# A decoder kernel with hand-laid tables: a new order of steps on five engines and of its PSUM pairs

## The chip, the cores and the metric

The kernel runs on one core of a Trainium2 chip. The core has a tensor engine (TensorE, PE in the profile; its weight loads are PEld), a vector engine (VectorE, DVE), a scalar engine (ScalarE, ACT), GpSimd (POOL), and a sync engine (SyncE, SP) that here only issues DMA transfers. Each runs its own instruction stream in order; they meet at semaphores. The metric is the device time of one execution, in microseconds (us). Lower is better.

## The reference, cut to what matters

Four decoder layers of three sublayers each are applied to `x` (64 sequences, 128 tokens, 128 channels). Each sublayer is followed by a residual and a layer norm:

```
x = _layernorm(x + _L0_attn_ref(x, ...))      # linear recurrence with a delta rule
x = _layernorm(x + _L0_xattn_ref(ctx_1024, x, ctx_1024, ...))   # 16 heads of 8 channels, 77 context rows
x = _layernorm(x + _L0_ffn_ref(x, gate_w, w1, w2))              # 8 experts, top 32 tokens each
x = _layernorm(x + _L1_attn_ref(...))         # 8 heads of 128, latent keys and values, causal
x = _layernorm(x + _L1_xattn_ref(...))        # cross attention with a mask
x = _layernorm(x + _L1_ffn_ref(...))          # fp4 quantized gate, up and down
...                                           # L2: attention, cross attention, mixture with low-rank tokens
...                                           # L3: rotary attention, relu cross attention,
                                              #     conv + attention + 8 gated experts of width 512
```

Nothing of this computation is changed. The same instructions run before and after.

## The kernel before

A first phase, the opening (about 375 us), solves the recurrence's triangular systems for all sequences and prepares weights. It isn't touched. Then comes the decoder phase. It takes the 64 sequences as 16 batches of 4. Three groups of buffers (`g0`, `g1`, `g2`, class `Group`) are in use at once: group n works through batches n, n+3, n+6, ..., one after another, and each visit is a *turn*. Group 0 has six turns, the other two have five.

Each engine's work on a batch is a Python generator that yields after each *step*: a few instructions that end with an increment of the group's semaphore for that engine. `whole_tensor`, `whole_scalar`, `whole_vector`, `whole_gpsimd` and `whole_sync` string the batches of a group together. The order in which an engine takes the three groups' steps is not found by a planner at build time. It stands in a table, `ORDER`: a digit per step says whose step comes next, and `in_order` obeys:

```
def in_order(programs, order):
    for who in order:
        next(programs[who], None)
```

So within one group the steps never change places. Only how the three groups are interleaved on an engine is free. SP has five programs: the three groups' loads and stores (digits 0, 1, 2) and two streams of expert weights, `a` for layer 0 and `b` for layer 3 (`stream_sync`, line 3044), 256 KB a piece into four places each. A piece waits until the matmuls that read the place's last content are done. Since SP runs in order, whatever stands behind a waiting step waits too.

At the end of a turn the group's SP program does these steps in this order: the store of the output (`store_sync`, L3024, after the last layer norm, "end normal"), then the next batch's loads (`loads_sync`): key mask (L2995), the dots (L2998), the context (L3002), the transposed input xT (L3006, into `qa`), the recurrence's result z in four DMAs (L3011) and the input x (L3015, into `o`).

On TensorE the new turn starts with *rec v* (L1764), which waits for xT, then *rec q* (L1767), *rec weights* (L1772, also waits for z and for ScalarE), and *rec y* (L1778). GpSimd adds a bias to x (*rec base*, L1843), VectorE adds rec y to it (*rec sum*, L1377), and the layer norm follows.

The attention sublayers use the same steps for each of 4 sequences: scores (L1599), two row maxima on VectorE (L1703), tops turned (L1611), scores shifted by the maximum (L1626), two exponentials on ScalarE (L1679), weighted values (L1649), by tokens (L1660). Lines 1599 and 1626 use 32 rows of the array per matmul and L1649 32 columns; the others use all of it, in the profile `128*128`. L2759 to L2806 are the gated experts of the last layer, L1986 and L1996 the experts of the first.

The second table, `GIVEN`, is a list of pairs of digits. It hands four pairs of PSUM banks in turn to the stages of the three groups (`give_banks`); a stage's first matmul waits until the pair's last reader is done (`take_banks`).

Of the kernel before, what the change touches and what calls it, by code (L numbers as in the profile page):

```python
# [224 lines left out]
def memory_layouts(w):  # L225
# [39 lines left out]
        "00101010202010210120020000201000010200020010110010112121211121221211121212201012012002100022000200010010"  # L265
        "00102021010000101101121121010100100101121101011001100100012020201001101101012002010121010211012212121111"
        "21120112021012201001021220220002102220210002010012102212211212111121222121112122211021002002020002222101"
        "12212110110122202020212012122020202220200202220202001202110100001001001010011010010100110101000110110110"
        "00110120012010220221221012001011010010111010201010110102111211000001011102120021010010101000101210100010"
        "20002020001211010110220212112221211212221211122012010011101221012101012020020202000220202000222020110120"  # L270
        "12202101220210102110010102021010001001100100200100201002000101000100200100100102001000002010010000010000"
        "10010010000212122121121210021021011011011010111021102011101100101110110002101110100011011002010101111102"
        "01101211010110010021001020021100120020020200000201102111102200002002220020020002010210020100120112020201"
        "01020120021021001011010010111010001011101001010211000122222101020210020020202211222211201122112102022112"
        "10100210201110101101200201211022000102202100012022002022021020201220120202220220020222020002202220200022"
        "02200101022022122011002101121021120110120120120210112011010102112212212212010000101121222111101001011101"
        "00221012100022020220002022001210120112011012100200222021222212010220021011021201010100101101000101110100"
        "01011102120121011021202212212222022122012102210022022022011002100200100110100100010010121002001020210020"
        "02120010010020010020022002212211021221201202012020212012212102102121002100200200200122112111222212121222"
        "12121212001011100101001110100112012212212022012010110001012020002101002112201201012121211212212111212221"  # L280
        "21112121220102102212020100002000201200120012021100100121021211210121110210012112012111211212021002001202"
        "01212112101011201220120020102102120120102002112110212010210001011011012012110121102102211011002020200002"
        "00002202001210122211212112221211202002120020012010122112110212101021121202110201201120202022020020222020"
        "00202220200012012010202011211011011011211210111012022101210201202212122102221020220220221022122000121202"
        "20212101202022022212112212211011002102120120110120210201102101010101122122122212012221001101022012211101"
        "01011101010101220200022020220002002012101012101210121202020220102212102202010212101202201010100101101000"
        "10111010001011102021020101221112022022202210122010220120120210200200202002200020010012010001001010102120"
        "01201110210021021012100100200212011021221202200102212210201201221221220122102102000200200200121212111222"
        "21212122212121212001010110101001110100112012210021221202211011000120020121001201210202010012121211212212"
        "11121222121112122210101210122002200000020202001021002021002101022120100102101112212110110211021012212112"  # L290
        "01121020121121121010110110210122010201012012020020121121201200121201200101100110111011201021202002021101"
        "10002022020002022101210222012112121221212122012002010012000122121112102111101021120122002012120202022020"
        "02022202000202220200022101201020011211111101121102101112021111211021102120220022021222102200202202220120"
        "00120212010122020220222122011001202102101102210110110220210210210210112221212211201202210221212021001121"
        "22210111101011101010101220202002020220002022100101021011201211202222000201212221020220201011021201010100"
# [149 lines left out]
    "13001223231122100203202011110223122302112002230020030221202001122112130302231102110002101200110321000013"  # L445
    "03222111122310022311212110102312030122102203101312212103200300212300011022232311021020021001012302100112"
    "12001103001321222111120012032301231020231210222011130220020121011312012022022000010022010000011301012300"
    "2300220223230300")

# [3053 lines left out]
```

## Time and profile before

| | |
|---|---|
| median of 3 runs | 5209.06 us (5198.81 to 5213.58) |
| the profiled execution | 5213.06 us |
| its span, first to last instruction | 5211.0 us |
| PE, DVE, ACT, POOL busy | 88%, 63%, 48%, 15% |
| PE busy from 420 us on | 4332.10 of 4791.00 us |

Busy shares count instructions in execution. In the decoder phase TensorE is nearly always busy, and the others wait for it and it for them in turn. The granted clock of TensorE is given as a share of full speed.

### The profile page before, as it was taken

What the parts mean: (1) busy time and instruction counts of PE and PEld (TensorE: products, weight loads), DVE (VectorE), ACT (ScalarE), POOL (GpSimd) and SP (SyncE); (2) the same over time, 40 slices, a digit from 0 to 9 for tenths busy, and PEclk for the clock granted to TensorE, in tenths of its full rate; (3) what the DMA queues carried; (4) which work ended last, traced back from release to release, by engine and by line L of the source; (5) the groups of instructions that cost most, each with busy time, mean ns of one, the idle gap of its engine ahead of it and who ended that gap; (6) DMA issues with size and microseconds to landing.
All of it is one profiled execution on the core that took longest, in us unless ns stands there. A gap on an engine that the chain in (4) does not pass through costs nothing.

```text
span 5211.0 us, 128498 instructions
## 1 busy us (share of the span) xinstructions
PE 4591.7 (88%) x54601; PEld 3382.8 (65%) x54601; DVE 3270.9 (63%) x8433; ACT 2486.6 (48%) x5062; POOL 786.2 (15%) x841
## 2 busy tenths in 40 slices
PE   5668988999898989899898989999998989898877
PEld 4336756677676767676676767676676767676554
DVE  6654587655657575756757575756657575757552
ACT  3324655535545455544545454544545454554431
POOL 5551210111011110101011111101011111101000
PEclk7668999999999999999999999999999999999987
DMA  2131100012010101111010101011000101010000
GB/s 65 29 89 51 61 2 2 4 55 59 28 34 19 56 21 48 29 40 37 22 42 15 56 21 50 25 44 35 26 30 21 56 23 50 23 40 24 14 23 29
DMA packets 154184, 181.62 MB, mean 35 GB/s; under 512 B 62890, under 2 KB 82450, under 8 KB 152850
## 3 DMA queue, kind: packets, MB, share of 16 engines
q1 hardware_dynamic: 153618, 173.41, 11.2%
q8 instruction: 437, 7.16, 0.6%
q14 instruction: 129, 1.06, 0.1%
HBM read 162.50 MB, written 10.55 MB: 33 GB/s over the span
## 4 chain that ended last, share of the span: by engine, by line
PE 66%; DVE 14%; ACT 6%; issue 3%; DMA 1%; POOL 1%; SPq 1%; POOLq 0%; DVEq 0%; ACTq 0%
PE g_pair L2774 9%; PE g_pair L2759 9%; PE g_pair L1599 6%; PE g_pair L1649 5%; DVE g_tops L1703 5%; PE g_pair L1626 5%; ACT g_keys_exps L1679 3%; PE g_pair L1996 2%; PE g_pair L1986 2%; PE g_pair L1433 2%; PE g_pair L1611 1%; PE g_pair L1660 1%; PE g_pair L2360 1%; PE g_pair L2060 1%; PE g_pair L1569 1%
## 5 line engine op out<-in xcount | busy, mean ns | idle before, releaser
L1679 ACT ACTIVATE g_keys_exps<-g_pair 128x1024 f32<-128x1024 f32 (+1 forms) x768 | 746.4, 1018 | 570.6 <-PE g_pair L1626 569.1
L1703 DVE TENSOR_REDUCE g_tops<-g_pair 128x8 f32<-128x1024 f32 (+1 forms) x768 | 749.9, 1006 | 335.1 <-PE g_pair L1599 332.8
L1412 POOL TENSOR_TENSOR g_rstd<-g_rstd,minus_half 128x4 f32<-128x4 f32 x224 | 234.8, 1049 | 3325.2 <-DVE g_rstd L1394 3319.0
L2774 PEld LDWEIGHTS g_pair<-region,g_keys_exps 128*128 128x128 f32 x4096 | 510.5, 192 | 120.1 <-issue 109.7
L2759 PE MATMUL g_pair<-g_xT,region 128*128 128x512 f32 x1024 | 545.1, 614 | 8.5 <-ACT g_keys_exps L2787 4.5
L2774 PE MATMUL g_pair<-region,g_keys_exps 128*128 128x128 f32 x4096 | 547.5, 278 | 2.9 <-DVE g_base L2806 2.9
L1649 PE MATMUL g_pair<-g_keys_exps,g_v 77*32 77x128 f32 (+1 forms) x12288 | 438.2, 286 | 70.6 <-DVE g_tops L1703 62.6
L1626 PE MATMUL g_pair<-g_qa,g_keys_exps 32*77 32x128 f32 (+1 forms) x12288 | 449.6, 284 | 46.0 <-DVE g_o L1724 28.7
L1599 PE MATMUL g_pair<-g_keys_exps,g_qa 32*128 32x256 f32 (+1 forms) x6144 | 394.1, 371 | 96.9 <-ACT g_keys_exps L1679 80.2
L1626 PEld LDWEIGHTS g_pair<-g_qa,g_keys_exps 32*77 32x77 f32 (+1 forms) x12288 | 386.1, 171 | 142.9 <-DVE g_o L1724 58.9
L1649 PEld LDWEIGHTS g_pair<-g_keys_exps,g_v 77*32 77x32 f32 (+1 forms) x12288 | 328.3, 114 | 178.9 <-DVE g_tops L1703 118.4
L1599 PEld LDWEIGHTS g_pair<-g_keys_exps,g_qa 32*128 32x128 f32 x6144 | 262.3, 192 | 206.5 <-ACT g_keys_exps L1679 130.9
L2787 ACT ACTIVATE g_keys_exps<-g_pair,region 128x512 f32<-128x512 f32 x256 | 176.0, 688 | 445.5 <-PE g_pair L2759 445.0
L2799 DVE TENSOR_SCALAR g_keys_exps<-g_pair,region 128x512 f32<-128x512 f32 x256 | 191.1, 747 | 308.5 <-PE g_pair L2759 308.0
L1673 ACT ACTIVATE g_oT_sc<-g_pair 128x256 f32<-128x256 f32 x384 | 147.1, 383 | 322.3 <-PE g_pair L1649 321.6
L1706 DVE TENSOR_TENSOR g_qa<-g_qa,g_pair 128x256 f32<-128x256 f32 x384 | 160.7, 419 | 201.9 <-PE g_pair L1611 199.4
L1421 ACT ACTIVATE g_x<-g_x,g_shift,g_rstd 128x128 f32<-128x128 f32 x384 | 173.0, 489 | 173.3 <-DVE g_shift L1398 173.0
L2155 POOL TENSOR_TENSOR g_keys_exps<-g_keys_exps,g_small 128x512 f32<-128x512 f32 x128 | 133.6, 1064 | 549.9 <-DVE g_small L2180 549.8
L2139 ACT ACTIVATE g_keys_exps<-g_pair,g_small 128x128 f32<-128x128 f32 x512 | 180.4, 379 | 52.3 <-DVE g_small L2169 51.7
L1611 PE MATMUL g_pair<-consts_sb,g_tops 128*128 128x128 f32 x768 | 159.5, 290 | 50.8 <-DVE g_tops L1703 47.9
L2759 PEld LDWEIGHTS g_pair<-g_xT,region 128*128 128x128 f32 x1024 | 157.8, 192 | 49.3 <-issue 41.2
L1660 PE MATMUL g_pair<-consts_sb,g_oT_sc 128*128 128x128 f32 x768 | 163.5, 299 | 21.8 <-ACT g_keys_exps L1679 11.2
(379 smaller groups left out, 8554.2 us busy)
## 6 DMA issues: line engine op xcount, KB each, us to landing
region<-L_w_in SPq DMA_DIRECT2D x512, 256.0 KB, 3.0
region<-xT_in SPq DMA_DIRECT2D x16, 256.0 KB, 2.7
z_scratch<-m_z SPq DMA_DIRECT2D x4, 1024.0 KB, 5.9
g_qa<-xT_in SPq DMA_DIRECT2D x16, 256.0 KB, 3.9
g_oT_sc<-z_scratch SPq DMA_DIRECT2D x64, 64.0 KB, 3.2
g_o<-x_in SPq DMA_DIRECT2D x16, 256.0 KB, 3.8
out<-g_x SPq DMA_DIRECT2D x16, 256.0 KB, 2.3
setup_weights<-prepared_in SPq DMA_DIRECT2D x1, 2589.5 KB, 10.6
```

Source lines behind the costliest of these rows:

```text
L1412: e.tensor_tensor(g.rstd[:, :], g.rstd[:, :], g.s["minus_half"], ALU.pow).then_inc(*b.gpsimd(st + " rstd"))
L1599: ins = e.matmul(bank[r][:, 2 * nk * t:2 * nk * (t + 1)].rearrange("p (i k) -> p i k", i=2), g.qa[rows, t, n, :], g.km[rows, n, t, :, 0:nk ...
L1611: ins = e.transpose(bank[2][:, t * T:(t + 1) * T], top_rows(g, t), g.k["ident"])
L1626: ins = e.matmul(bank[r][0:nk, u * T:(u + 1) * T], g.km[rows, n, t, i, 0:nk], g.qa[rows, t, n, :], start=not masked, stop=not masked or u ...
L1649: ins = e.matmul(b.bank[st][0][32 * u:32 * u + 32, k * T:(k + 1) * T], g.v[0:nk, n, 8 * i + 4 * k + u, :], g.p[0:nk, 2 * i + k, u, :], sta ...
L1660: ins = e.transpose(b.bank[st][1][:, k * P:(k + 1) * P], outputs_of(g, n)[:, k, :], g.k["ident"])
L1679: e.activation(g.p[0:nk, 2 * k:2 * k + 2, :, :].rearrange("p g u q -> p (g u q)"), b.pair[st][k][0:nk, :, :].rearrange("p r c -> p (r c)") ...
L1703: e.tensor_reduce(top_columns(g, k), src, AX, ALU.max).then_inc(*b.vector(f"{st} top {n} {k}"))
L2139: ins = e.activation(g.lat_e[n % 2][:, j, :], bank[2 + kv][:, h * T:(h + 1) * T], ACT.Exp, bias=g.small[:, 40 + j:41 + j], accum_out=g.lat ...
L2759: e.matmul(bank[0][:, :], weights.part(f"w1 {x}", c), g.xT, start=True, stop=True).then_inc(*b.tensor(f"f3 hidden {k}"))
L2774: ins = e.matmul(bank[1][:, n * D:(n + 1) * D], g.gated_hid[:, x % 2, c, n * T:(n + 1) * T], weights.part(f"w2 {x}", c), start=c == n == 0 ...
L2799: e.tensor_scalar(g.gated_hid[:, x % 2, k % HC, :], b.bank["ex"][0][:, :], g.w["f3_b1"][:, k:k + 1], 0.0, ALU.add, ALU.max).then_inc(*b.ve ...
```

## The change

All entries of `ORDER` and `GIVEN` are laid anew; no function is touched. The tables keep their length and the count of each digit: 5040 steps on TensorE, of which 1353 places hold another digit, 971 of 3472 on ScalarE, 2456 of 7728 on VectorE, 134 of 528 on GpSimd, 173 of 624 on SP. A step stands on average half a place (TensorE) to two places (SP's loads) from where it stood. One line of SP's table stands for all:

```diff
     "sync": (
-        "00002212aa12abb01112ba0b21aaaaaaaaaaaaaaaaaaaaaaaaaaaaaaaaaaaaaaaaaaaaaaaabbbbbbbbbbbbb000bb0000bbbbbbbb"
+        "00000111120b22a21ba2a1a2aaaaaaaaaaaaaaaaaaaaaaaaaaabaaabaaaaaaaaaaaaaaaaaabbbbbbbbbbbbb000000bb0bbbbbbbb"
...
 GIVEN = (
-    "02201102112003221303110211030213200323111011002203012220101201031220010013122301221001110201231120231110"
+    "00201102032011132203111120020313020311102311002222002313120101001201231013012011020223120320022112131102"
```

**SP at the decoder's start.** `g0`, `g1`, `g2` are the groups; `region` is the place of weight pieces. Before, from the eleventh issue on:

```order
L3006 DMA g2_qa<-xT_in 128x512
L3054 DMA region<-L0_w1_in 128x512
L3054 DMA region<-L3_w1_in 128x512 x2
L3011 DMA g0_oT_sc<-z_scratch 128x4x32 x4
L3002 DMA g1_ctxT<-ctxT_in 128x308
L3006 DMA g1_qa<-xT_in 128x512
L3011 DMA g1_oT_sc<-z_scratch 128x4x32 x4
L3011 DMA g2_oT_sc<-z_scratch 128x4x32 x4
L3054 DMA region<-L3_w2_in 128x512
L3054 DMA region<-L0_w1_in 128x512
L3015 DMA g0_o<-x_in 128x4x128
```

This piece is preceded by ten more issues (g0's mask, dots, context and xT, small loads of g1 and g2, two weight pieces). After, from the very first issue to the same load of g0's x:

```order
L2995 DMA g0_mask_int<-key_mask_in 1x308
L2998 DMA g0_kq_dot<-s_scratch 128x4
L3002 DMA g0_ctxT<-ctxT_in 128x308
L3006 DMA g0_qa<-xT_in 128x512
L3011 DMA g0_oT_sc<-z_scratch 128x4x32 x4
L2995 DMA g1_mask_int<-key_mask_in 1x308
L2998 DMA g1_kq_dot<-s_scratch 128x4
L3002 DMA g1_ctxT<-ctxT_in 128x308
L3006 DMA g1_qa<-xT_in 128x512
L2995 DMA g2_mask_int<-key_mask_in 1x308
L3015 DMA g0_o<-x_in 128x4x128
```

Group 0's z and x have moved ahead of the loads of group 2 and of all weight pieces: x is the eleventh row instead of the twenty-first.

**TensorE at the decoder's start.** Before, from its first matmul (`g_pair` are PSUM pairs):

```order
L1764 MATMUL g_pair2<-rec_vo,g0_qa 128x128 x4
L1767 MATMUL g_pair2<-g0_qa,region 128x512
L1764 MATMUL g_pair1<-rec_vo,g1_qa 128x128 x4
L1772 MATMUL g_pair2<-g0_qa,g0_oT_sc 128x128 x4
L1767 MATMUL g_pair1<-g1_qa,region 128x512
L1778 MATMUL g_pair2<-g0_keys_exps 128x128 x4
L1772 MATMUL g_pair1<-g1_qa,g1_oT_sc 128x128 x4
L1474 MATMUL g_pair2<-g0_ctxT,region 128x308
```

After:

```order
L1764 MATMUL g_pair0<-rec_vo,g0_qa 128x128 x4
L1767 MATMUL g_pair0<-g0_qa,region 128x512
L1772 MATMUL g_pair0<-g0_qa,g0_oT_sc 128x128 x4
L1764 MATMUL g_pair1<-rec_vo,g1_qa 128x128 x4
L1778 MATMUL g_pair0<-g0_keys_exps 128x128 x4
L1474 MATMUL g_pair2<-g0_ctxT,region 128x308
```

Group 0's rec weights (L1772) stands ahead of group 1's rec v (L1764), and its rec y (L1778) ahead of group 1's rec q (L1767). Group 0 has changed its pair from 2 to 0.

**SP at the end of a turn**, here group 1's first. Before; the store is the third row:

```order
L3054 DMA region<-L3_w1_in 128x512
L3054 DMA region<-L0_w2_in 128x512 x7
L3024 DMA out<-g1_x 128x4x128
L3054 DMA region<-L3_w1_in 128x512
L3054 DMA region<-L3_w2_in 128x512
L2995 DMA g1_mask_int<-key_mask_in 1x308
L2998 DMA g1_kq_dot<-s_scratch 128x4
L3054 DMA region<-L0_w1_in 128x512 x2
L3002 DMA g1_ctxT<-ctxT_in 128x308
L3006 DMA g1_qa<-xT_in 128x512
L3054 DMA region<-L0_w1_in 128x512
```

After:

```order
L3054 DMA region<-L3_w2_in 128x512
L3054 DMA region<-L0_w1_in 128x512
L3024 DMA out<-g1_x 128x4x128
L3054 DMA region<-L0_w1_in 128x512 x2
L2995 DMA g1_mask_int<-key_mask_in 1x308
L2998 DMA g1_kq_dot<-s_scratch 128x4
L3002 DMA g1_ctxT<-ctxT_in 128x308
L3006 DMA g1_qa<-xT_in 128x512
L3011 DMA g1_oT_sc<-z_scratch 128x4x32 x4
```

Between the store (L3024) and the load of xT (L3006) stood four weight pieces (L3054), now two. Over the 13 ends of a turn that are followed by another turn, 23 pieces stood there before and 5 now. The result's load z (L3011) follows xT at once, and the weight pieces come after it.

## Rows read from the trace of the kernel before

**Rows 1.** Busy time by stretch: start:end, length, busy per engine, clock, DMA share, GB/s
```profile
410.00:700.00 290.00, 256.20 (x3010) 198.20 (x3009) 172.54 (x457) 161.14 (x404) 43.83 (x40) 0.89 0.15 45
...
1600.00:2200.00 600.00, 549.38 (x6565) 410.86 (x6564) 394.53 (x1040) 309.72 (x593) 74.86 (x70) 0.99 0.11 34
```

**Rows 2.** Who waited for whom: total us, times, longest us
```profile
PE g_pair L1599 <- ACT g_keys_exps L1679: 80.2, 99, 3.4
...
PE g_pair L1649 <- DVE g_tops L1703: 62.6, 125, 1.8
...
PE g_pair L1611 <- DVE g_tops L1703: 47.9, 50, 2.5
```

**Rows 3.** The same for 420 to 5211 us, TensorE and the first-input load
```profile
PE g_pair L1764 <- DMA g_qa<-xT_in: 31.6, 13, 5.0
```

**Rows 4.** Timeline of SP, group 1's first turn: start, us, line, tiles
```profile
1265.62 0.39 SPq L3024 DMA_DIRECT2D out<-g_x  x1
1266.06 0.99 SPq L3054 DMA_DIRECT2D region<-L_w_in  x2
...
1269.23 0.43 SPq L3006 DMA_DIRECT2D g_qa<-xT_in  x1
...
1271.01 2.62 SPq L3011 DMA_DIRECT2D g_oT_sc<-z_scratch  x4
```

**Rows 5.** Timeline of TensorE there; in brackets the idle time before
```profile
1274.76 2.08 PE L1764 MATMUL g_pair<-rec_vo,g_qa 128*128 128x128 f32 x8 [5.00 <-DMA g_qa<-xT_in]
```

**Rows 6.** Timeline of SP, group 0's last turn: no weights in between
```profile
4502.78 0.40 SPq L3024 DMA_DIRECT2D out<-g_x  x1
...
4504.49 0.43 SPq L3006 DMA_DIRECT2D g_qa<-xT_in  x1
```

**Rows 7.** Timeline of TensorE there
```profile
4507.41 1.16 PE L1764 MATMUL g_pair<-rec_vo,g_qa 128*128 128x128 f32 x8 [1.17 <-DMA g_qa<-xT_in]
```

**Rows 8.** Chain that ended last: start, us, what
```profile
1269.23 5.48 DMA g_qa<-xT_in
...
2454.99 6.28 DMA g_qa<-xT_in
```

**Rows 9.** By stretch: 4 us after the load landed, four turns of the thirteen
```profile
1130.20:1134.20 4.00, 3.91 (x16) 2.76 (x17) 0.00 (x0) 0.69 (x1) 1.40 (x2) 0.62 0.55 155
1274.70:1278.70 4.00, 3.94 (x44) 3.45 (x44) 1.83 (x4) 0.00 (x0) 0.00 (x0) 0.60 0.65 157
...
2165.00:2169.00 4.00, 3.93 (x25) 2.91 (x26) 0.71 (x2) 0.00 (x0) 1.67 (x3) 0.57 0.40 92
...
3927.80:3931.80 4.00, 3.95 (x14) 2.45 (x18) 1.02 (x3) 0.13 (x1) 0.30 (x1) 0.50 0.72 203
```

**Rows 10.** Chain at the decoder's start: start, us, what
```profile
391.56 4.02 DMA g_o<-x_in
...
395.65 1.10 POOL g_base L1843
...
396.85 0.70 DVE g_x L1377
```

**Rows 11.** Timeline of TensorE at the start
```profile
377.88 2.04 PE L1764 MATMUL g_pair<-rec_vo,g_qa 128*128 128x128 f32 x8 [7.39 <-DMA g_qa<-xT_in]
...
387.95 2.04 PE L1764 MATMUL g_pair<-rec_vo,g_qa 128*128 128x128 f32 x8 [6.32 <-DMA g_qa<-xT_in]
389.79 1.92 PE L1772 MATMUL g_pair<-g_qa,g_oT_sc 128*128 128x128 f32 x8
...
393.20 1.38 PE L1778 MATMUL g_pair<-g_keys_exps 128*128 128x128 f32 x8
```

**Rows 12.** Timeline of TensorE in a full stretch
```profile
2022.87 1.06 PE L2774 MATMUL g_pair<-region,g_keys_exps 128*128 128x128 f32 x8
...
2025.58 1.11 PE L1626 MATMUL g_pair<-g_qa,g_keys_exps 32*77 32x128 f32 x32
2026.62 1.16 PE L2774 MATMUL g_pair<-region,g_keys_exps 128*128 128x128 f32 x8
```

More of the change, by code:

```diff
@@ new lines @@
+        "12210112021012210100201220200022012220120002010012122012211212111121222121112122121021002002002020220121"
+        "12212110110122221020022012122020202220200202220200021202110100001001001010011010010100110101000110110110"
+        "00110102012010220221221012001011010010111021001010110102112111000001011102120021010010120100010110100010"
+        "20020020001211010110220212112221211212221212112010100111201221012101012020020202000220202000222020101121"
+        "02021201222010120110010102021010001001100102001002000102000100100102001000001010020001002000100100010010"
@@ L313 @@
+        "22220000002220220022020002202000202202000000002022020000000000000000000000000000000000000000000000000000"
         "000000000000000000000000000000000000000000000000"),
     "scalar": (
[L315 to L317 removed]
@@ new lines @@
+        "01100120120120222100011111111100022222120020102100012221222222210110102000112010211120020000000202211111"
+        "02112201022220111011111110002222201200102200011221222222221011002001011021021211002000000002221211111021"
+        "22012202010111111111000022221220201210000221221222222101100002011012102111202000000000222121101112201212"
+        "22010011111111100020222212200012100021221222222121110002000112010211210002000000202211202220220200000002"
+        "02000000"),
+    "sync": (
+        "00000111120b22a21ba2a1a2aaaaaaaaaaaaaaaaaaaaaaaaaaabaaabaaaaaaaaaaaaaaaaaabbbbbbbbbbbbb000000bb0bbbbbbbb"
+        "bbbbbaabaaaaaaaaaaabba1aa11111b1aaaaaaaaaaaabbbabababbbbbbabbbbb2222222aaaaaaaaaaaabbbbbabbabbbbab00000b"
+        "00abbbaaaaaaaaaaaabababbbbabbbbbb11a1111bb1bbaaaaaaaaaaaaababbbbbbaabbbbb222222bb2bbaaaaaaaabaaaaaabbbba"
+        "abbbbbbbbbb0000000baaaaaaaaaaaabbbaababbbbabbbbb11111b1bb1aaaaaaaaaaaababbaabbbbbbbbbb222222b2bbaaaaaaaa"
+        "aaaaababbbabbbbbaabbb000000bbb0baaaaaaaaaaaabaabbbbbaabbbbbb1b11b11bb11aaaaaaaaaaababaaabbabbbbbbbbbb222"
+        "222b2baaaaaaaaaaaabaabababbbbbbbbb0000000bbaabaaaaaaaaaabbbbbbbbbbbbbbbbb1bbbbbbbbbbbbbbbb2bbbbbbbbbbbb0"),
@@ L452 @@
+    "21130012012110211310230223211012011010220301221123122320012301000123001022001112000123232201001212230110"
+    "11120022032100130003221211231112002311221223102101201301201302112220232002021103230221002100000101002322"
+    "2301010200000300")
 BATCH = {
```

327 lines of the change are left out of this document (154 added, 173 removed).

## The prediction

> **What bounds the kernel now.** I first read the busy shares by stretch. From 420 us on TensorE is busy 4332 of 4791 us, in a typical stretch 549 of 600 us at a granted clock of 0.99 [rows 1]. So TensorE bounds the kernel. The matmuls themselves can't go; what a new order can take away is TensorE's 459 us of idle time after 420 us (4791.00 - 4332.10, the table of the section on time), the idle time of the start, and time in which TensorE runs at less than its full clock.
>
> Next I read who waits for whom. The idle time is spread thin. The largest entries are the scores waiting for ScalarE's exponentials, 80.2 us in 99 waits, and weighted values and tops waiting for VectorE's maxima, 62.6 and 47.9 us in 125 and 50 waits [rows 2]. These are hand-overs inside an attention, half a microsecond to a microsecond each. One entry is of another kind: rec v, the first matmul of a new turn, waits for the load of xT in all 13 later turns, 31.6 us together, up to 5.0 us at once [rows 3].
>
> Then I read SP's timeline at such a place. The store of group 1's output is issued at 1265.62, two weight pieces stand behind it (0.99 us for the two), two more further on, and xT is issued only at 1269.23, 3.6 us after the store [rows 4]. TensorE idles 5.00 us for it [rows 5]. In the turn in which nothing stands between, the way from store to xT is 4504.49 - 4502.78 = 1.7 us, the matmul starts 2.9 us after the issue, and TensorE idles 1.17 us [rows 6, 7]. Between weight pieces the load itself is slower too: 5.48 and 6.28 us from issue to landing in the chain [rows 8].
>
> The wait has a second price. rec v after the wait of 5.00 us takes 2.08 us for its eight matmuls, after the wait of 1.17 us it takes 1.16 [rows 5, 7]. The stretches of 4 us behind the landing show the granted clock: 0.62, 0.60, 0.57 and 0.50, the lower of TensorE's two levels (1.2 GHz) for part or all of the time [rows 9]. Seven of the 13 turns show this, four of them with 0.50; the other six stay at 1.00.
>
> **The change part by part.** No instruction is added or removed, and the steps of one group keep their order, so every term is about time between steps.
>
> *Loads at the end of a turn.* Of 23 weight pieces that stood between store and xT over the 13 turns, 5 are left. Each took about 0.47 us of SP (0.99 for two plus the gap [rows 4]), so xT is issued 18 x 0.47 = 8.5 us earlier in sum, and without their traffic it should land in 2.9 us rather than 5.5 to 6.3 [rows 7, 8]. rec v also moved on TensorE. I counted in both orders, with the trace's duration of each step, the matmuls between the last step on which the store depends and rec v: 5.5 us on average before (3.7 to 6.6), 7.2 after (6.6 to 8.2). The way that this has to cover is 1.7 + 2.9 = 4.6 us in the undisturbed case [rows 6, 7], plus up to 1 us for the last normalization steps. 6.6 us cover it in every turn. So the idle 31.6 us can go whole, and with it the low clock: over 4 us each, 4 x (0.38 + 0.40 + 0.43 + 4 x 0.50) = 12.8 us [rows 9]. Together 44 us at most. I don't take it whole. While TensorE stood, VectorE and ScalarE caught up with their queues, and some of the hand-overs behind rec v will now be late in its place: the bounds are 0 and 44, and since the attention hand-overs in flight there are of 0.5 to 1 us (80.2/99, 62.6/125 [rows 2]), about one per turn, I give back 13 x 1.0 = 13 us and take -31 us.
>
> The Trainium skill weighs against part of this. Its page "DMA: Bandwidth & Descriptors", section "Anatomy of one DMA", puts a DMA's time at a fixed 2.0 us, mostly its completion, and bytes over 436 GB/s, measured for DMAs issued by GpSimd; for 256 KB that makes an estimate of 2.6 us whatever stands around it. The undisturbed landing agrees, those of 5.48 and 6.28 us don't [rows 7, 8], and the measurement decides. By the rule only the issue and the cover would count, and the turn at 2451, whose cover stays at 6.6, would keep some 2 us of its wait; the sum would be about 3 us smaller.
>
> *The start.* Group 0's x was issued at 391.56, landed 4.02 us later, and the chain of waits runs through it: bias on GpSimd 1.10 us, rec sum at 396.85 [rows 10]. It is now the eleventh SP step. From its present start the first four issues end at about 375.3; z's four take 2.6 (as in [rows 4]), five small ones about 0.4 each. That gives an issue near 379.8, landing near 383.8, bias done by 385. On TensorE rec v and rec q end at 381.6; then rec weights 1.92, rec v of group 1 about 2.0 and rec y 1.38 us follow [rows 11], the end is near 387.3. rec sum would start at 387.4 rather than 396.85: 9.5 us earlier. Up to 700 us TensorE is busy 256.20 of 290.00 us [rows 1], so what follows is partly bound by TensorE and not by this chain. I take -7 of bounds 0 and -10. The first two uses of pair 0 (group 0, then group 2) now follow each other, so group 2's rec v waits for rec sum; before it ran after 398, so this is covered.
>
> *Changes of array shape.* The order has 1897 neighbours of unlike shape (whole array, 32 rows, 32 columns) where it had 1921. A group of eight matmuls behind a 32-row group takes 1.16 us, behind others 1.06 [rows 12]. 24 x 0.10 = -2 us. With a row going into the 32-row shape costing as much again it is -5; zero is the other bound.
>
> *Everything else.* 1353 of TensorE's places changed, nearly all by a swap with a neighbour. I compared the cover (matmul time between a step and the step that waits for its result) by kind: scores behind the exponentials 1.93 us before and 1.96 now in the own attentions, tops turned 2.58 and 2.61, x0 to x2's weighted values 1.68 and 1.52. Waits for a hand-over with under 1 us of cover are 788 where they were 750. That is a wash: 0, with bounds from -20 to +20 (38 more by 0.5 us each, rounded [rows 2]). The weight pieces that now come after z have at least 7.4 us of matmuls before their use in layer 3, and landed in about 3: nothing.
>
> Sum: -31 - 7 - 2 = -40 us. The profiled execution took 5213.06 us, its span 5211.0; minus 40 is 5173. That execution lies 4.0 us above the median of the runs, 5209.06, so the median becomes **5169 us**. This measurement can't tell less than about 0.3% (16 us) from no change.
>
> **The rivals.**
> *The waits only move.* TensorE reaches the next hand-over earlier and waits there. For it: ScalarE and VectorE work through the same queues, and some waits of [rows 2] are bound by their chains. Against it: they are less loaded than TensorE, and the clock comes back in any case. If three quarters of the 31.6 us are given back and half of the clock's 12.8 remains, the gain is 8 + 6, with 2 for the start: -16, 5193 us, with a range to 5209.
> *Slower: thin covers break.* The place is scores against VectorE's maxima in the attentions. 38 more hand-overs have under 1 us of cover. If each exposes its longest of 1.8 us [rows 2] instead of 0.5, that is +68 against -40: 5237 us. It decides from 40/38 = 1.05 us each. Against it is that the mean of 125 such waits is 0.5.
> *More than that.* The small hand-overs improve as well, because the order was laid around real durations: 10% off 459 us of idle time, -46, with the -40: 5123 us. Against it: the covers are alike.
> *The tables don't do what they say,* no effect of waits and loads: 5209. The order speaks against it, since SP's loads have moved; I count it with the first rival.
>
> **How the numbers follow.** The forecast case (5150 to 5190) gets 0.58, the larger gain 0.12, the moved waits 0.20, the slower case 0.10. The best sum by the bounds is -44 - 10 - 5 - 20 = -79, 5130; the range takes most of that and the first rival: 5138 to 5206. Faster by over 0.3% (under 5193.4) has the forecast, the larger gain and a fifth of the moved waits: 0.74. Within 0.3%: 0.16. Slower: 0.10.
>
> **What would show it.** In the profile after, the waits of L1764 for xT fall from 31.6 us to under 8 from 420 us on, and the stretches behind them show a clock of 1.00. At each end of a turn SP issues xT 1.7 us after the store, where no weights stand between. At the start rec sum begins near 387, and TensorE's busy share up to 700 us rises. The waits of L1599, L1649 and L1611 stay within a tenth of 80, 63 and 48 us. If the xT waits are gone and those have grown by 25 us or more, the first rival is right; if they have grown by over 40, the slower one. If xT still lands late, my landing time of 2.9 us is wrong.

## The result, and the profile after

| | before | after |
|---|---|---|
| median | 5205.02 us (4 runs, 5198.81 to 5213.58) | 5134.37 us (4 runs, 5133.33 to 5134.58) |
| ratio, with its 95% interval | | 0.9863 [0.9846, 0.9880] |
| the profiled execution | 5213.06 us, span 5211.0 | 5134.53 us, span 5132.4 |
| PE busy from 420 us to the end | 4332.10 of 4791.00 us | 4293.94 of 4712.40 us |

The change takes off 71 us. The forecast was 40, and 5134.4 lies just under the range of 5138 to 5206. The profiled execution of before was 8 us slower than its median, so the two traces differ by 79 us. From 420 us on, TensorE's idle time fell from 459 to 418 us and its busy time by 38 us: the same matmuls took less time. The granted clock accounts for nearly all of that. From 420 us on it stood at the lower of its two levels for 404 us before and for 334 after, and 70 us less at half speed are worth 35.

The same stretches as in [rows 1], after; columns as there. The busy share up to 700 us is what it was, at a higher clock:

```profile
410.00:700.00 290.00, 256.83 (x3031) 200.00 (x3032) 185.66 (x478) 166.80 (x416) 40.69 (x39) 0.92 0.15 47
1600.00:2200.00 600.00, 556.13 (x6554) 416.92 (x6547) 396.65 (x1039) 307.85 (x591) 73.56 (x68) 0.97 0.11 34
```

Who waited for whom, after, for [rows 2]. The three large entries hardly moved; an entry of L1764 on xT [rows 3] is no longer there:

```profile
PE g_pair L1599 <- ACT g_keys_exps L1679: 80.2, 92, 2.7
PE g_pair L1649 <- DVE g_tops L1703: 58.6, 121, 1.8
PE g_pair L1611 <- DVE g_tops L1703: 51.4, 51, 2.5
```

SP and TensorE at group 1's first end of a turn, after (timelines: start, us), for [rows 4, 5]. Two weight pieces still stand ahead of xT; rec v comes 5.5 us behind its issue, without idle time before it, and at full clock:

```profile
1234.58 0.39 SPq L3024 DMA_DIRECT2D out<-g_x  x1
1235.02 1.00 SPq L3054 DMA_DIRECT2D region<-L_w_in  x2
...
1237.25 0.43 SPq L3006 DMA_DIRECT2D g_qa<-xT_in  x1
1237.72 2.08 SPq L3011 DMA_DIRECT2D g_oT_sc<-z_scratch  x4
```

```profile
1242.71 1.06 PE L1764 MATMUL g_pair<-rec_vo,g_qa 128*128 128x128 f32 x8
```

The decoder's start, after, in the chain that ended last (start, us, what), for [rows 10, 11]. The chain no longer runs through x, but through TensorE. rec sum is the row of L1377:

```profile
372.70 3.07 DMA g_qa<-xT_in
...
375.90 2.05 PE g_pair L1764 x8
...
380.44 2.08 PE g_pair L1772 x8
382.51 1.71 PE g_pair L1764 x8
384.22 1.06 PE g_pair L1778 x8
...
385.30 0.70 DVE g_x L1377
```

Where the time went can be read from the stores of the groups' outputs, one at each end of a turn. These are the first and the thirteenth in SP's timeline; of before (the thirteenth, at 4502.78, is in [rows 6]):

```profile
1123.56 0.39 SPq L3024 DMA_DIRECT2D out<-g_x  x1
```

and after, with the load of xT behind the first:

```profile
1099.45 0.39 SPq L3024 DMA_DIRECT2D out<-g_x  x1
...
1101.16 0.43 SPq L3006 DMA_DIRECT2D g_qa<-xT_in  x1
...
4423.16 0.39 SPq L3024 DMA_DIRECT2D out<-g_x  x1
```

Up to the first store 24 us went (2 of them already in the opening, which the change doesn't touch), in the twelve turns between first and thirteenth (3379.2 us before, 3323.7 after) 56 us, and behind it 1 us was added. So the gain is in two parts, a start and a long middle, and both are larger than forecast.

### The profile page after: what moved, and what is told of

Same layout as the page of the kernel before. It is cut to its first block, busy times and chain, and to the rows that moved or that the text cites. A ratio compares the mean times of both kernels' runs of the same rounds, so it can differ in the third digit from the quotient of the medians.

```text
span 5132.4 us, 128497 instructions
## 1 busy us (share of the span) xinstructions
PE 4564.4 (89%) x54601; PEld 3364.1 (66%) x54601; DVE 3280.6 (64%) x8433; ACT 2485.0 (48%) x5062; POOL 780.2 (15%) x841
## 3 DMA queue, kind: packets, MB, share of 16 engines
q14 instruction: 129, 1.06, 0.1%
## 4 chain that ended last, share of the span: by engine, by line
PE 64%; DVE 15%; ACT 6%; issue 6%; POOL 2%; DMA 0%; SPq 0%; POOLq 0%; DVEq 0%; ACTq 0%
PE g_pair L2774 8%; PE g_pair L2759 8%; PE g_pair L1599 6%; DVE g_tops L1703 5%; PE g_pair L1649 5%; PE g_pair L1626 5%; ACT g_keys_exps L1679 4%; PE g_pair L1996 2%; PE g_pair L1986 2%; PE g_pair L1611 2%; PE g_pair L1433 1%; PE g_pair L1660 1%; PE g_pair L2060 1%; PE g_pair L2360 1%; PE g_pair L1569 1%
## 5 line engine op out<-in xcount | busy, mean ns | idle before, releaser
L1412 POOL TENSOR_TENSOR g_rstd<-g_rstd,minus_half 128x4 f32<-128x4 f32 x224 | 233.0, 1041 | 3305.4 <-DVE g_rstd L1394 3304.8
L1649 PE MATMUL g_pair<-g_keys_exps,g_v 77*32 77x128 f32 (+1 forms) x12288 | 437.8, 286 | 67.7 <-DVE g_tops L1703 58.6
L1599 PE MATMUL g_pair<-g_keys_exps,g_qa 32*128 32x256 f32 (+1 forms) x6144 | 390.0, 368 | 99.9 <-ACT g_keys_exps L1679 80.2
L2155 POOL TENSOR_TENSOR g_keys_exps<-g_keys_exps,g_small 128x512 f32<-128x512 f32 x128 | 131.8, 1048 | 559.6 <-DVE g_small L2180 559.6
L1611 PE MATMUL g_pair<-consts_sb,g_tops 128*128 128x128 f32 x768 | 160.7, 292 | 54.6 <-DVE g_tops L1703 51.4
```

The costliest lines, as they stand in the source:

```text
L1412: e.tensor_tensor(g.rstd[:, :], g.rstd[:, :], g.s["minus_half"], ALU.pow).then_inc(*b.gpsimd(st + " rstd"))
L1599: ins = e.matmul(bank[r][:, 2 * nk * t:2 * nk * (t + 1)].rearrange("p (i k) -> p i k", i=2), g.qa[rows, t, n, :], g.km[rows, n, t, :, 0:nk ...
L1611: ins = e.transpose(bank[2][:, t * T:(t + 1) * T], top_rows(g, t), g.k["ident"])
L1649: ins = e.matmul(b.bank[st][0][32 * u:32 * u + 32, k * T:(k + 1) * T], g.v[0:nk, n, 8 * i + 4 * k + u, :], g.p[0:nk, 2 * i + k, u, :], sta ...
```

## Experiments

Every kernel ran in five rounds beside the kernel before. "us" is the ratio's distance from 1 times the median of before in the same runs (5204.4 to 5211.4 us). An interval of the ratio of 0.0015 to each side is 8 us. A single profile tells less: between the first and the thirteenth store start_only has before's tables and took 3369.85 us, 9.4 us less than before itself. Differences of that size between single profiles are no evidence.

| kernel | median | ratio [95%] | us |
|---|---|---|---|
| start_only | 5181.59 | 0.9960 [0.9946, 0.9973] | -21 |
| rest_only | 5151.68 | 0.9901 [0.9885, 0.9917] | -52 |
| start_sp | 5200.02 | 0.9976 [0.9963, 0.9990] | -12 |
| start_engines | 5203.17 | 0.9992 [0.9979, 1.0006] | -4 |
| start_and_sp | 5165.06 | 0.9925 [0.9911, 0.9940] | -39 |
| pieces_back | 5197.22 | 0.9967 [0.9955, 0.9978] | -17 |
| xt_early | 5180.53 | 0.9959 [0.9943, 0.9974] | -21 |
| after_xt_early | 5143.37 | 0.9864 [0.9846, 0.9883] | -71 |
| turn_ends | 5175.31 | 0.9918 [0.9900, 0.9936] | -43 |
| between (with SP's start, see below) | 5193.22 | 0.9966 [0.9951, 0.9981] | -18 |
| ends_engines | 5168.74 | 0.9915 [0.9900, 0.9931] | -44 |
| ends_sp_early | 5180.05 | 0.9936 [0.9920, 0.9952] | -33 |
| ends_pool | 5171.70 | 0.9927 [0.9904, 0.9949] | -38 |
| ends_pe_pool | 5180.52 | 0.9942 [0.9922, 0.9962] | -30 |
| ends_dve_act | 5194.76 | 0.9967 [0.9952, 0.9982] | -17 |
| ends_pe | 5197.83 | 0.9983 [0.9968, 0.9998] | -9 |

### The start alone, and all but the start

start_only has the changed tables up to about 440 us (49 steps of TensorE, 46 of ScalarE, 75 of VectorE, 14 of GpSimd, 63 of SP and 11 pairs) and before's behind them. rest_only is the reverse. First rows of TensorE's table, start_only against before:

```diff
     "tensor": (
-        "00101010202010210120020000201000010200020010110010112121211121221211121212201012012002100022000200010010"
+        "00010012021002020012201001000001010000202100101010112121211121221211121212201012012002100022000200010010"
...
```

rest_only against the changed kernel:

```diff
     "tensor": (
-        "00010012021002020012201001000001010000202100101010112121211121221211121222101012012001200022000200100100"
+        "00101010202010210120020000201000010200020010110010112121211121221211121222101012012001200022000200100100"
...
```

> The changed tables up to about 440 us (49 steps of TensorE, 46 of ScalarE, 75 of VectorE, 14 of GpSimd, 63 of SP, 11 pairs), behind that the tables of before. Theory: the earlier start is kept whole, -20 us against before (5185), all of it before the first batch's x0 y. Rival (what the prediction had): TensorE is busy enough up to 700 us that only 7 us of it are left at the end (5198).

> The reverse: the start of before, the changed tables behind it. Theory: idle time for xT (31.6 us) and low clock behind it (13 to 19 us) go, nothing is given back: -50 us (5155). Rival (the waits move on): -31 us or less (5174 or more). If the two halves add up, this and start_only together make the -71 us.

21 and 52 us add up to the whole 71 within their intervals. In start_only rec sum of the three groups starts at 384.24, 397.32 and 399.36 us (VectorE's timeline):

```profile
384.24 0.69 DVE L1377 TENSOR_TENSOR g_x<-g_base,g_pair 128x512 f32<-128x512 f32 x1 [0.35 <-PE g_pair L1778]
...
397.32 0.69 DVE L1377 TENSOR_TENSOR g_x<-g_base,g_pair 128x512 f32<-128x512 f32 x1 [0.26 <-POOL g_base L1843]
399.36 0.69 DVE L1377 TENSOR_TENSOR g_x<-g_base,g_pair 128x512 f32<-128x512 f32 x1 [1.34 <-PE g_pair L1778]
```

in before at 396.85, 404.76 and 411.60:

```profile
396.85 0.69 DVE L1377 TENSOR_TENSOR g_x<-g_base,g_pair 128x512 f32<-128x512 f32 x1 [4.42 <-POOL g_base L1843]
404.76 0.69 DVE L1377 TENSOR_TENSOR g_x<-g_base,g_pair 128x512 f32<-128x512 f32 x1 [1.76 <-PE g_pair L1778]
411.60 0.68 DVE L1377 TENSOR_TENSOR g_x<-g_base,g_pair 128x512 f32<-128x512 f32 x1
```

Each group's rec sum is 7 to 13 us earlier, of which 1.1 us are an earlier beginning of the decoder in that execution (first rec v at 376.74, before 377.88 [rows 11]). The stretches of 60 us at the start tell the rest, start_only (length, busy time of PE, PEld, DVE, ACT, POOL, then the clock):

```profile
360.00:420.00 60.00, 42.91 (x498) 32.02 (x499) 22.69 (x62) 22.42 (x39) 21.60 (x31) 0.75 0.33 92
420.00:480.00 60.00, 51.61 (x852) 41.47 (x840) 32.63 (x95) 32.12 (x52) 4.17 (x4) 0.91 0.08 24
```

and before:

```profile
360.00:420.00 60.00, 36.40 (x353) 28.11 (x357) 19.65 (x53) 13.72 (x25) 20.60 (x30) 0.67 0.38 103
420.00:480.00 60.00, 51.21 (x817) 37.31 (x809) 26.68 (x73) 30.16 (x47) 4.17 (x4) 0.76 0.01 2
```

TensorE was as busy behind 420 us in before, but at a mean clock of 0.76 instead of 0.91. From 360 to 480 us the clock stood at the lower level for 68 us in before and for 40 in start_only. Compared step by step on VectorE, start_only leads by 12.6 us at group 0's rec sum and by 19 at 480 us, and about as much at 1000. A busy engine at 0.76 had room that I had counted as full.

### The start by engines

start_sp changes only SP's first 63 steps; start_engines changes the engines' first steps and the 11 pairs and leaves SP's. Against before:

```diff
     "sync": (
-        "00002212aa12abb01112ba0b21aaaaaaaaaaaaaaaaaaaaaaaaaaaaaaaaaaaaaaaaaaaaaaaabbbbbbbbbbbbb000bb0000bbbbbbbb"
+        "00000111120b22a21ba2a1a2aaaaaaaaaaaaaaaaaaaaaaaaaaabaaabaaaaaaaaaaaaaaaaaabbbbbbbbbbbbb000bb0000bbbbbbbb"
...
```

start_engines (GpSimd's row stands for all):

```diff
     "gpsimd": (
-        "00010121201222101000200100001101111111202222212222010211000210001011021100101202110100000020220121000011"
+        "00001202121122101000200100001101111111202222212222010211000210001011021100101202110100000020220121000011"
...
```

> The tables of before with the first 63 steps of SP's changed table alone. start_only, all engines up to 440 us, gave -21 us. TensorE still does group 1's rec v ahead of group 0's rec weights, so group 0 waits for group 1's xT as well. Theory: group 1's xT lands about 5 us earlier and x about 11, which gives half or more of it: -10 to -15 us (5195).

> The first steps of the changed tables on TensorE, ScalarE, VectorE and GpSimd and the first 11 pairs, SP's table of before. Group 0's z is issued as before (landing at 386), its x at 391.6. Theory: rec sum waits for x as before, so 0 to -3 us (5205). Rival (the order on TensorE is what counts): -10 us or more.

SP's order carries most of the start: -12, the engines' -4, and their sum is -21 within the intervals. Counted from the first rec v, group 0's rec sum starts 19.0 us later in before, 18.6 in start_engines, 8.8 in start_sp and 7.5 in start_only. With the engines' order alone TensorE waits 4.79 us for z, and group 2's rec v waits 5.12 us for rec sum, a wait which the prediction had called covered (timeline of start_engines; it is covered only if x comes early too):

```profile
386.56 2.05 PE L1772 MATMUL g_pair<-g_qa,g_oT_sc 128*128 128x128 f32 x8 [4.79 <-DMA g_oT_sc<-z_scratch]
...
397.45 2.05 PE L1764 MATMUL g_pair<-rec_vo,g_qa 128*128 128x128 f32 x8 [5.12 <-DVE g_x L1377]
```

### The loads of xT

xt_early keeps before's tables and issues the next turn's xT in the same step as the store, ahead of the store's wait (`load_xT` holds the wait for the tile and the issue, taken out of `loads_sync`). after_xt_early is the changed kernel with the same edit:

```diff
-    for b in batches:
+    for b, after in zip(batches, batches[1:] + [None]):
         yield from loads_sync(e, b, dram, b.index * SEQS)
+        if after:
+            load_xT(e, after, dram)
         yield from store_sync(e, b, dram, b.index * SEQS)
```

> The tables of before; in the code alone, the next batch's xT is issued by SP just ahead of the wait for the store of the batch before, as soon as that batch's last attention has read its queries. It removes the 13 waits for xT and nothing else. Theory (nothing is given back): idle 31.6 and clock 13 us go, -44 us (5161). Rival (waits move on, three quarters come back): -16 us (5189). My prediction's term was -31 (5174).

> The kernel after, with xT issued ahead of the store as in xt_early. The changed kernel has no wait for xT left, so the theory says no change, within 5 us of 5134. Rival (crowding of SP's queue at the ends still costs it time, through dots, z and x, which move up by one issue): 5 to 15 us faster (5124).

All 31.6 us of waits for xT are gone and 21 us come of it (13 to 30 by the interval), nearer to the rival's 16 than to the theory's 44. So rest_only's -52 met its expectation of -50 by luck: something was given back, and something else was gained. On top of the changed order the edit brings nothing: there no wait for xT was left. What stands in its place is in the waits of xt_early from 420 us on:

```profile
PE g_pair L2094 <- POOL g_keys_exps L2155: 6.5, 5, 4.3
PE g_pair L1772 <- DMA g_oT_sc<-z_scratch: 6.5, 4, 2.4
```

In before the first of these was 1.8 us and the second was none. All of TensorE's waits in that view add up to 432 us in before and 415 in xt_early: of the 31.6 us about 15 came back, 11 of them in these two rows and the rest in small entries. Two late loads stood behind the late xT: z, and x. How x reaches L2094 is seen on GpSimd in xt_early at group 1's first end:

```profile
1268.45 1.09 POOL L1843 TENSOR_TENSOR g_base<-g_o,region 128x512 f32<-128x512 f32 x1 [4.99 <-DMA g_o<-x_in]
1269.63 1.24 POOL L1847 TENSOR_SCALAR g_mask<-g_mask_int 1x308 f32<-1x308 int32 x1
1270.95 2.04 POOL L2155 TENSOR_TENSOR g_keys_exps<-g_keys_exps,g_small 128x512 f32<-128x512 f32 x2
```

and on TensorE there, where 4 us at half the clock follow:

```profile
1272.14 2.02 PE L2094 MATMUL g_pair<-consts_sb,g_keys_exps 128*128 128x128 f32 x8 [4.32 <-POOL g_keys_exps L2155]
```

```profile
1272.10:1276.10 4.00, 3.96 (x19) 3.77 (x20) 1.78 (x4) 0.00 (x0) 0.89 (x1) 0.50 0.02 4
```

The wait of 5.00 us of [rows 5] became one of 4.32, with the low clock behind it as before. GpSimd held rec base (L1843) at the head of its queue until x had landed, and L2155 of another group, whose inputs were ready, stood behind it. VectorE had made the last input of L2155 at 1264 us:

```profile
1263.98 0.20 DVE L2180 RECIPROCAL g_small<-g_small 128x8 f32<-128x8 f32 x1 [0.62 <-ACT g_keys_exps L2139]
```

### SP's order alone

start_and_sp is start_only with the rest of SP's changed table too. pieces_back is before, with only the weight pieces moved behind z at the 13 ends of a turn (27 of them). start_and_sp against start_only:

```diff
     "sync": (
...
-        "bbbbaaabaabaaaaaaa1bb11aa11a1a1aaabaaaaaaaaababaabbbbabbbbbb2b2b222b2b2aaaaaaaaaaaabababbbbabbbbbbb00b0b"
+        "bbbbbaabaaaaaaaaaaabba1aa11111b1aaaaaaaaaaaabbbabababbbbbbabbbbb2222222aaaaaaaaaaaabbbbbabbabbbbab00000b"
...
```

pieces_back against before:

```diff
     "sync": (
...
-        "bbbbaaabaabaaaaaaa1bb11aa11a1a1aaabaaaaaaaaababaabbbbabbbbbb2b2b222b2b2aaaaaaaaaaaabababbbbabbbbbbb00b0b"
+        "bbbbaaabaabaaaaaaa111111bbaaaa1aaabaaaaaaaaababaabbbbabbbbbb222222bbbb2aaaaaaaaaaaabababbbbabbbbbbb00000"
...
```

> start_only, and SP's whole table from the change, the other engines' tables of before behind the start. Tells the part of the loads' issue (fewer weight pieces ahead of xT) from the part of rec v's later place on TensorE. Theory, issue and crowding carry half: xT waits fall from 31.6 to about 12 us, -20 for the start and -25 for the loads (5160). Rival (the cover of matmuls carries it): -20 and -8 (5177), xT waits still over 20 us.

> The tables of before but for SP's: at the 13 ends of a turn the weight pieces between store and z stand behind z. Tells the late issue and the crowding by weight pieces from the rest. The same idea with the whole SP table gave -18 us and xT waits of 15.3 us. Theory: -15 to -18 us (5188), xT waits about 15 us. Rival (it was SP's other moves, x and z): under 8 us.

-39 (between the theory's -45 and the rival's -28) against start_only's -21, and -17 against before, agree: SP's order behind the start is worth 17 to 18 us without any change on the engines. The waits for xT are still 15.3 and 8.8 us, so it gives nearly as much as taking xT out of the queue ahead of the store's wait.

### Around the ends of a turn, and between them

turn_ends changes all tables in 13 windows from 25 us ahead of the last normalization step to 45 us behind it (142 places of TensorE); between has the changed tables outside these windows and, on the engines, only behind 450 us (1182 places of TensorE). SP's table in it is the changed one from the first step on, so it contains the whole edit of start_sp. Its expectation takes it for the complement behind 450 us, which it isn't for SP.

```diff
     "tensor": (
...
-        "12202101220210102110010102021010001001100100200100201002000101000100200100100102001000002010010000010000"
+        "12202101220210102110010102021010001001100100200100201002000101000100200100100102001000002010010000010010"
...
```

between against before:

```diff
     "tensor": (
...
-        "12212110110122202020212012122020202220200202220202001202110100001001001010011010010100110101000110110110"
+        "12212110110122221020022012122020202220200202220200021202110100001001001010011010010100110101000110110110"
...
```

> The changed tables of all engines and pairs only in 13 windows, from 25 us before the end of a turn to 45 us behind it (142 places of TensorE, 74 of SP); the tables of before elsewhere, the start too. xt_early gave -21 us of the -52 behind the start, so about 30 us have another source. Theory 1 (they too come from the turns' ends: z, x, dots and the steps of the recurrence stand better): -45 to -50 us (5157). Theory 2 (they come from the many swaps between the ends): -20 us (5184), as xt_early.

> The complement of turn_ends behind 450 us: the changed tables only between those windows (1182 places of TensorE). Theory 1: 0 to -7 us (5200). Theory 2: -30 us (5174), with the waits for xT still about 31 us. If both add up, the two make -52.

A tenth of TensorE's moved places carries -43 of rest_only's -52. The -18 of between (-10 to -26) is not what the other nine tenths bring, for SP's order at the start is in it. Its rec sum comes 8.2 us behind the first rec v, as in start_sp (8.8) and not as in before (19.0):

```profile
380.15 2.05 PE L1764 MATMUL g_pair<-rec_vo,g_qa 128*128 128x128 f32 x8 [7.46 <-DMA g_qa<-xT_in]
```

```profile
388.39 0.69 DVE L1377 TENSOR_TENSOR g_x<-g_base,g_pair 128x512 f32<-128x512 f32 x1 [1.31 <-PE g_pair L1778]
```

start_sp alone gave -12. What is left for the moves between the ends is about -5, give or take 11: it can't be told from nothing. That fits theory 1 (0 to -7) and rest_only: -43 and -5 make -48 of its -52.

### The engines' order against SP's, at the ends

Both kernels start from xt_early. ends_engines takes turn_ends' tables except SP's, ends_sp_early takes only SP's.

```diff
     "tensor": (
...
-        "12202101220210102110010102021010001001100100200100201002000101000100200100100102001000002010010000010000"
+        "12202101220210102110010102021010001001100100200100201002000101000100200100100102001000002010010000010010"
...
```

```diff
     "sync": (
-        "00002212aa12abb01112ba0b21aaaaaaaaaaaaaaaaaaaaaaaaaaaaaaaaaaaaaaaaaaaaaaaabbbbbbbbbbbbb000bb0000bbbbbbbb"
+        "00002212aa12abb01112ba0b21aaaaaaaaaaaaaaaaaaaaaaaaaaaaaaaaaaaaaaaaaaaaaaaabbbbbbbbbbbbb000000bb0bbbbbbbb"
...
```

> turn_ends with SP's table of before, and xT issued ahead of the store as in xt_early. So at the turns' ends TensorE, VectorE, ScalarE and GpSimd follow the changed tables, while z, dots and x are issued where they were. turn_ends gave -43 us, xt_early -21. Theory (the 20 us more are the engines' order: rec v and its followers stand where their inputs are ready, so the work that they displaced covers other hand-overs): -40 us (5168). Rival (they are the earlier z, dots and x): -21 us (5187).

> The reverse: the engines' and pairs' tables of before, SP's table of turn_ends, xT early. Theory: like xt_early, -21 us (5187). Rival (earlier z, dots and x): -35 to -40 us (5170).

Behind xT's 21 us the engines' order brings 23 us more, SP's (earlier z, dots and x) 12 us more, each with some 11 us to either side. Together they bring no more than the first alone (turn_ends, -43; it has SP's table in place of the edit in the code, and waits for xT of 2.2 us). The waits of xt_early, 6.5 us on z and 6.5 on L2155, are none and 1.8 in ends_engines, 4.0 and 3.9 in ends_sp_early (where -33 bears out the rival of the expectation). So I read them as two cures of one thing: the late loads of z and x either come earlier, or what stands behind them is taken out of their way. The busy time of TensorE in the 13 stretches from 20 us ahead of each of the first 13 stores to 50 us behind it, one sum line per kernel. Before:

```profile
sum 910.00, PE 755.14 PEld 548.07 DVE 688.05 ACT 476.40 POOL 154.00; mean PE 58.09 PEld 42.16 DVE 52.93 ACT 36.65 POOL 11.85
```

xt_early:

```profile
sum 910.00, PE 766.98 PEld 561.20 DVE 712.80 ACT 485.86 POOL 153.43; mean PE 59.00 PEld 43.17 DVE 54.83 ACT 37.37 POOL 11.80
```

ends_engines:

```profile
sum 910.00, PE 780.69 PEld 568.52 DVE 719.67 ACT 489.68 POOL 157.62; mean PE 60.05 PEld 43.73 DVE 55.36 ACT 37.67 POOL 12.12
```

after:

```profile
sum 910.00, PE 782.33 PEld 572.22 DVE 731.96 ACT 496.40 POOL 160.20; mean PE 60.18 PEld 44.02 DVE 56.30 ACT 38.18 POOL 12.32
```

TensorE stood idle for 154.9, 143.0, 129.3 and 127.7 us of the 910.

### Which engine's order

Again from xt_early, with turn_ends' table of one or two engines: GpSimd's (41 places), TensorE's (142), both, and VectorE's with ScalarE's (622). ends_pool against xt_early:

```diff
     "gpsimd": (
-        "00010121201222101000200100001101111111202222212222010211000210001011021100101202110100000020220121000011"
+        "00010121201222101000200100001101111111202222212222010211000210001011021100101202100110000200222011000010"
-        "10000120210120222100011111111100022222012200121000012221222222210110100200112010211120020000000202211211"
+        "01100120210120222100011111111100022222120200121000012221222222210110102000112010211120020000000202211111"
...
```

ends_pe, and with it ends_pe_pool:

```diff
     "tensor": (
...
-        "12202101220210102110010102021010001001100100200100201002000101000100200100100102001000002010010000010000"
+        "12202101220210102110010102021010001001100100200100201002000101000100200100100102001000002010010000010010"
...
```

ends_dve_act (ScalarE's row stands for both):

```diff
     "scalar": (
...
-        "20010011020100121001201111002121001221022120001000001022210010001010010000101000010012222020100000002201"
+        "20010011020100121010021111001210021221021220001000010022210010001010010000101000010012222020100000002201"
...
```

> The order before, the next xT issued ahead of the store's wait, and GpSimd's changed order around the 13 ends of a turn alone (41 places): there GpSimd's products L2155 stand ahead of rec base L1843, which waits for the load of x. Theory A (late loads hold GpSimd, and TensorE waits behind it): the wait of 4.3 us on L2155 at group 1's end goes, the waits on L2155 fall from 6.5 us to under 2, and the time comes out some 4 to 6 us under the kernel with xT early alone (ratio about 0.9950 to before). Theory B (the gain behind the xT term is the order of TensorE among short hand-overs): nothing, 0.9959.

> The same base (order before, xT early), and TensorE's changed order around the 13 ends of a turn alone (142 places). Theory A: a fifth of the 22 us at most, ratio 0.9950 to 0.9959. Theory B: most of the 22 us that the engines' order around the ends brought together, ratio 0.9915 to 0.9930.

> The same base, and TensorE's and GpSimd's changed order around the 13 ends. Theory A: as GpSimd's alone, about 0.9950. Theory B: as TensorE's alone plus those 4 us, 0.9910 to 0.9925. If it stays above 0.9940 while all four engines' order together gave 0.9915, the order is a whole and no engine's part carries it.

> The same base, and the changed order of VectorE and ScalarE around the 13 ends alone (622 places). Both theories: they only follow TensorE's order, so without it nothing or a loss: ratio 0.9955 to 0.9990. If it gains by over 10 us against the kernel with xT early alone (under 0.9940), the gain lies in VectorE's and ScalarE's queues.

GpSimd's order brings 17 us on top of xT's 21, some three to four times the expectation of theory A. With 12 and 8 us to either side of the two kernels the difference lies between 2 and 31 us, so its sign is shown and its size isn't. The wait on L2155 fell as theory A had it,

```profile
PE g_pair L2094 <- POOL g_keys_exps L2155: 2.2, 4, 1.3
```

the wait for z didn't (7.1 us), and all of TensorE's waits fell by 8 us, from 415 to 406. Theory B falls: it expected 0.9915 to 0.9930 of TensorE's order alone, which gives 0.9983 and so loses 12 against xt_early. In six of the 13 ends GpSimd's rec base now stands behind a step of another group that it had stood ahead of: three times a normalization's inverse root (L1412), twice the base of a sum, once L2155. In two others it is the other way round. The place of one such end, xt_early at 4459, GpSimd:

```profile
4466.99 1.09 POOL L1843 TENSOR_TENSOR g_base<-g_o,region 128x512 f32<-128x512 f32 x1 [4.17 <-DMA g_o<-x_in]
4468.04 1.02 POOL L1412 TENSOR_TENSOR g_rstd<-g_rstd,minus_half 128x4 f32<-128x4 f32 x1
```

VectorE and TensorE there:

```profile
4469.09 0.16 DVE L1398 SCALAR_TENSOR_TENSOR g_shift<-g_mean_var,g_rstd 128x4 f32<-128x4 f32 x1 [2.96 <-POOL g_rstd L1412]
```

```profile
4470.01 2.05 PE L1778 MATMUL g_pair<-g_keys_exps 128*128 128x128 f32 x8 [2.95 <-DVE g_keys_exps L1811]
```

ends_pool, the same end: GpSimd,

```profile
4458.20 1.01 POOL L1412 TENSOR_TENSOR g_rstd<-g_rstd,minus_half 128x4 f32<-128x4 f32 x1 [2.70 <-DVE g_rstd L1394]
4459.39 1.09 POOL L1843 TENSOR_TENSOR g_base<-g_o,region 128x512 f32<-128x512 f32 x1 [0.18 <-DMA g_o<-x_in]
```

and TensorE:

```profile
4460.73 1.13 PE L1778 MATMUL g_pair<-g_keys_exps 128*128 128x128 f32 x8 [0.66 <-DVE g_keys_exps L1811]
```

A chain of a load and three engines: GpSimd waits for x, the inverse root of another group behind it is late, VectorE waits 2.96 us for that and has L1811 behind it, and TensorE waits 2.95 us and then runs at half its clock (2.05 us instead of 1.13). The trace of before has the same chain at its last turn, behind the wait of [rows 7]. GpSimd, VectorE and TensorE there:

```profile
4511.18 1.09 POOL L1843 TENSOR_TENSOR g_base<-g_o,region 128x512 f32<-128x512 f32 x1 [4.70 <-DMA g_o<-x_in]
4512.23 1.02 POOL L1412 TENSOR_TENSOR g_rstd<-g_rstd,minus_half 128x4 f32<-128x4 f32 x1
```

```profile
4513.28 0.16 DVE L1398 SCALAR_TENSOR_TENSOR g_shift<-g_mean_var,g_rstd 128x4 f32<-128x4 f32 x1 [3.53 <-POOL g_rstd L1412]
```

```profile
4514.20 2.05 PE L1778 MATMUL g_pair<-g_keys_exps 128*128 128x128 f32 x8 [2.08 <-DVE g_keys_exps L1811]
```

TensorE's order alone, with the others' as they were, costs 12 us, and even with GpSimd's the pair is 8 us worse than GpSimd's alone (the intervals overlap; 0.9942 lies on the border that the expectation had set). With all four engines' orders it is -44, so TensorE's order seems laid for partners that have moved too. Which partner it lacks no run shows. VectorE's and ScalarE's alone do nothing that can be told (-17 against xt_early's -21).

## Why the prediction was wrong

The direction was right, the forecast 31 us short.

*Loads at the end of a turn, -31.* What it said of the loads holds: the waits for xT are gone, xT is issued 1101.16 - 1099.45 = 1.7 us behind the store where no weights stand between. It lands in 2.9 us in the median where it took 3.9, and the eight matmuls of rec v take 1.06 to 1.16 us in all 13 turns, the full clock. No turn keeps a wait, not even the one at 2451, for which the prediction had named some 2 us by a fixed landing time. The price didn't: without these waits the kernel gains 21, not 31 of 44 us. The give-back did not go to the attention hand-overs that I named; their three entries together fell by 2 us. 11 us of it are the waits for z and, over GpSimd's queue, for x. The rest isn't assigned, and the 21 itself has 8 us to either side. SP's order without the engines gives 17 to 18.

*The start, -7.* Measured -21. rec sum started at 385.3, against a forecast of 387.4; 2.0 us of that are an earlier first rec v, and counted from there it is 9.4 us against 9.5, so this chain was forecast rightly. The failing step is "up to 700 us TensorE is busy 256.20 of 290.00 us, so what follows is partly bound by TensorE": that busy time held matmuls at half clock, and the clock came back with the earlier start. Also I followed group 0's chain and not groups 1 and 2, which gained 7 and 12 us. The bound of -10 was the gain of one chain. TensorE's busy share to 700 us did not rise as announced.

*Changes of array shape, -2.* Not separated from the rest by any run.

*"That is a wash: 0" for everything else.* This is the step that failed most. rest_only's -52 less the 21 for xT leaves 31 us, beyond even its bound of 20. The engines' order around the ends of a turn brings 23 of them; of the engines' orders that were tried by themselves only GpSimd's gains, 17 (2 to 31). The moves between the ends bring some 5, if anything. I compared covers on TensorE only, by kind, over the whole kernel. For GpSimd, whose table had changed in 134 places and which is 15% busy, the prediction has no term: its part was put at nothing without a reason. The chain of a load and three engines could be read in the trace of before, at 4511 us.

*The rivals.* "The waits only move" said 5193 and was wrong for the whole, but half true of its own term: of the 44 us of waits and clock, xt_early shows 23 given back. "More than that" gave 5123 with 10% off the idle time; the idle time fell by 9% (459 to 418) and the time is nearer to it than to the forecast. But its reason isn't what happened: the small hand-overs stayed within a tenth (80.2, 58.6, 51.4 us). The slower case had nothing to show.

What stays open: whether the moves between the ends bring anything, which engines' orders must go together for the 23 us at the ends, and how these divide between idle time saved and clock.

## What to carry to other kernels

A step that waits for a load holds the whole in-order queue of its engine: for each such step, list what stands behind it and who waits for that, on the idle engines first. When one late load is taken off the critical path, look at the next loads of the same burst (here z and x behind xT) before pricing the gain. And busy time at a low clock is not a bound: read the clock of a stretch together with its busy share.

## What the runs showed of the hardware

The clock falls behind waits, whatever ended them: a load (5.00 us, [rows 5, 9]), GpSimd (4.32 us, 0.50 in the next 4 us) or VectorE (2.95 us, then eight matmuls in 2.05 us). It doesn't fall behind every one. Of the 13 waits for xT in before, the seven of 2.05 us and more were followed by a rec v of 1.32 to 2.08 us, the six of up to 1.98 us by one of 1.16. That is no general border: between 480 and 4760 us of that trace a fall also followed 24 of TensorE's 80 idle gaps of 1 to 2 us, and it followed 16 of the 17 longer ones.

Between 480 and 4760 us the granted clock stood at the lower level in 41 stretches, 263 us in all, before the change, and in 29 with 212 us after it. Part of that is spread between executions: start_only, which has before's tables there, shows 42 stretches with 232 us.

Where the clock is low differs between executions. At the decoder's start, over the same order and the same loads, the eight matmuls of rec weights took 2.08 us in the changed kernel and 1.16 in start_only, and rec sum came 9.4 and 7.5 us behind the first rec v.
